# Masks of a routed MLP as a penalty in PSUM instead of a multiplication, and the order of one batch's products

## The chip, the cores and the metric

The kernel runs on one core of a Trainium2 chip. The metric is the device time of one execution in microseconds; several executions are timed and their median is given. The profile comes from one further execution.

## The reference, cut to what matters

The input is x, 4 batches of 256 tokens with 256 features, and a context of 4 x 256 x 64. Two layers follow, each an attention and an MLP, each added to x through a tanh gate. The change touches the first layer's MLP and what stands around it:

```python
# first layer, attention: adjacency from the context
A = sigmoid(sim) * (sim >= 76th largest of its row)
A = (A + A.T) * 0.5                      # mixed with the identity, applied to layernorm(x)
# first layer, MLP: 16 blocks of 64 hidden units, each token keeps its best 4 blocks
prob = softmax(xf @ Wr.T + br)
mask = 1 at the 4 largest of 16, else 0  # per token
h = gelu(xf @ W1b) * mask[:, :, None]
y = h @ W2b
x = x + tanh(g_ffn[0]) * y
```

The second layer is a latent attention over 16 heads, done in pairs of heads, and a mixture of experts. Neither is edited.

## The kernel before, in words

The program is written out by hand for each engine: each has one queue of instructions in program order, and semaphores join them. A batch b (0 to 3) has two tiles of 128 tokens.

VectorE (lines 888 to 960) runs, for each batch, ten rounds on the similarity of the context, MAX8 (line 908) and MATCH_REPLACE8 (line 913), to find the 76th largest value of each row, and then writes the thresholded A (line 936), which raises `a_ok`. Between the rounds of batch b it does the rest of the work of earlier batches, at fixed rounds: `first(b-1)` (line 823, adds the attention to x and takes the statistics), `norm_inverse` and `norm_apply` (lines 90 and 98, write XN), `second(b-2)` (line 855, adds the MLP's y), `route(b-1)` (lines 837 to 847, writes the mask MK, 1 where a block is among the best four), and `rest` (line 864).

TensorE does, for batch b: `result(b-1, 0..3)`, the MLP's second product of the previous batch (line 630, accumulated in the bank YB, raises `y_ps`); `norm_turn`, the transpose of XN (line 107); the logits (line 665); four units, each the hidden values of four blocks, two times 128 of them, by 256 tokens (line 674, f32, eight matmuls), written in turn to two banks; behind each unit the masks of the unit before (line 613): for each of the four blocks a column of MK is spread over 64 columns as the stationary operand, the moving one is the f16 identity, and so a full mask of 128 x 512 comes out in the bank MB, eight f16 matmuls of 128 columns. Then `symmetric(b+1)`, the transposed sum A + A.T of the next batch (lines 589 and 590, waits for `a_ok`), the masks of the last unit, and for b of 1 and 2 `second_norm(b-1)`. In the last batch the products of the next attention stand between the units: `first_queries(k)` for k of 0 to 2 (line 243), `second_norm(2)` after the second unit and `result(3, n-2)` behind the third and fourth.

ScalarE takes each unit through the gelu (line 774) to one of two buffers GL in SBUF and copies each mask from PSUM to one of two buffers MS (line 781). In between stand the square roots of the norms (line 83), which need another table than the gelu, so that tables are loaded (ACT_TABLE_LOAD) four times in a batch.

POOL multiplies GL by MS into HT (line 481), 128 x 512 values a unit; HT is what the second product reads. In the last batch it also adds the rotated halves of the queries (`add_partners`, line 276), each behind one of these products. SyncE issues the swaps that these additions wait for (lines 267 and 268) once VectorE has rotated a group (`rotate_query`, lines 256 and 257).

After the last result TensorE does the first context product (lines 284 and 286), `next_fold(0)` (line 143), the turn of batch 3, `next_fold(1)`, and the attention begins.

## Time and profile before

| | us |
|---|---|
| median of 3 executions | 461.74 |
| lowest, highest | 461.54, 463.14 |
| profiled execution: its time | 463.19 |
| its span | 461.3 |
| TensorE busy | 435.8 (94%) |
| VectorE busy | 303.1 (66%) |
| ScalarE busy | 252.4 (55%) |
| POOL busy | 194.3 (42%) |

Views of the profile give times in us from the start of the span. PE is TensorE, PEld its weight loads, DVE VectorE, ACT ScalarE, SPq the queue of SyncE. A line of a timeline has the start, the time covered, the engine, the source line, the operation, output and inputs, shapes and the count of instructions merged into it (x8). Merged matmuls start one behind the other while their ends overlap, so the distance to the next start tells the cost. In square brackets stands the idle time before the line and what ended it. The program names buffers by their tensor: `wide` holds A, SIM and XA; `kc`, `ks`, `CT` and `XT` are also GL and MS here; `turned` and `HT` are the two buffers HT.

### The profile page before, as it was taken

The page shows a single profiled execution, that of the slowest core. Times are in us where ns is not written, and L with a number is a line of the kernel's source. Part 1 is how long each engine was busy: PE and PEld are TensorE (multiplying, and loading weights), DVE is VectorE, ACT ScalarE, POOL GpSimd, SP SyncE. Part 2 cuts the span into 40 slices and gives each one's busy share as a digit, 9 for nine tenths or more (in the row PEclk, how much of TensorE's full clock was granted, in tenths as well). Part 3 has the DMA queues.
Part 4 walks back from the last instruction along what each step waited for, and adds up shares of the span by engine and source line. Part 5 has one row for each costly group of instructions (what it writes and reads, how often), then busy time and mean ns, then how long its engine had stood idle before and what let it go on. Part 6 is the DMA issues. An engine that isn't in the chain of part 4 may idle for free. (4 is left out here: it accounts for less than half of the span.)

```text
span 461.3 us, 8845 instructions
## 1 busy us (share of the span) xinstructions
PE 435.8 (94%) x2723; PEld 278.3 (60%) x2723; DVE 303.1 (66%) x880; ACT 252.4 (55%) x629; POOL 194.3 (42%) x195
## 2 busy tenths in 40 slices
PE   5898998889988999999999999999999999989997
PEld 2586876777744555556555556555467784644476
DVE  3989799965247757677666677767744548546613
ACT  3584445444344776767677766677667342145510
POOL 1641404040434556555465754565643433744000
PEclk9995999999999999999999999999999988999999
DMA  7643000000204343442334333212200399889212
GB/s 243 195 122 87 25 0 2 1 1 7 64 0 99 77 101 82 97 119 66 93 77 107 92 73 98 59 43 58 70 23 2 111 309 312 227 183 274 74 36 92
DMA packets 61464, 43.81 MB, mean 95 GB/s; under 512 B 22971, under 2 KB 54518, under 8 KB 61430
## 3 DMA queue, kind: packets, MB, share of 16 engines
q1 hardware_dynamic: 60662, 41.04, 33.8%
q0 software_dynamic: 768, 2.36, 2.5%
q8 instruction: 17, 0.28, 0.2%
q14 instruction: 17, 0.14, 0.1%
HBM read 27.25 MB, written 2.23 MB: 64 GB/s over the span
## 5 line engine op out<-in xcount | busy, mean ns | idle before, releaser
L1208 POOL TENSOR_TENSOR W1T<-W1T,inv 128x512 f32<-128x512 f32 x64 | 66.5, 1040 | 79.4 <-DVE inv L1263 79.4
L1152 ACT ACTIVATE W1T<-ps,low 128x256 f32<-128x256 f32 x128 | 59.5, 470 | 30.8 <-DVE low L1257 30.8
L276 POOL TENSOR_TENSOR rot<-rot 128x512 f32<-128x512 f32 x48 | 61.0, 1271 | 26.7 <-DMA rot<-rot 26.7
L1257 DVE TENSOR_REDUCE low<-ps 128x2 f32<-128x512 f32 x64 | 44.1, 689 | 39.1 <-PE ps L1067 38.6
L1160 ACT ACTIVATE W2T<-ps 128x512 f32<-128x512 f32 x64 | 38.2, 597 | 7.2 <-PE ps L1075 5.2
L1075 PEld LDWEIGHTS ps<-ident,W1T 128*128 128x128 f32 x256 | 27.8, 141 | 23.7 <-issue 20.7
L1075 PE MATMUL ps<-ident,W1T 128*128 128x128 f32 x256 | 41.1, 283 | 0.9 <-POOL W1T L1208 0.8
L256 DVE TENSOR_TENSOR rot<-ps,sinq 128x512 f32<-128x512 f32 x48 | 33.2, 691 | 13.4 <-PE ps L243 11.2
L243 PE MATMUL ps<-XH,CH 128*128 128x512 f16 x96 | 36.4, 379 | 0.9 <-DVE XL L864 0.9
L243 PE MATMUL ps<-XL,CH 128*128 128x512 f16 x96 | 36.4, 379 | 0.0
L243 PE MATMUL ps<-XH,CL 128*128 128x512 f16 x96 | 36.4, 379 | 0.0
L1084 PE MATMUL ps<-W2T,KV 128*64 128x256 f32 x256 | 34.7, 392 | 0.0
L674 PE MATMUL ps<-XT,W1T 128*128 128x256 f32 x128 | 33.3, 410 | 0.0
L257 DVE TENSOR_TENSOR rot<-ps,cosq 128x512 f32<-128x512 f32 x48 | 32.6, 680 | 0.0
L1067 PE MATMUL ps<-KL,Q 128*128 128x256 f16 x128 | 31.4, 273 | 0.0
L1067 PE MATMUL ps<-KH,Q 128*128 128x256 f16 x128 | 31.4, 273 | 0.0
L674 PEld LDWEIGHTS ps<-XT,W1T 128*128 128x128 f32 x128 | 25.4, 205 | 4.3
L908 DVE MAX8 m<-work 128x8 f32<-128x256 f32 x72 | 26.7, 412 | 0.0
L913 DVE MATCH_REPLACE8 work<-m,work 128x256 f32<-128x256 f32 x64 | 25.7, 408 | 0.0
L1152 ACT ACTIVATION_READ_ACCUMULATOR W1T<-ps,low 128x1 f32 x128 | 25.3, 198 | 0.0
L134 PE MATMUL ps<-NH,wide 128*128 128x256 f16 x128 | 23.1, 273 | 1.0 <-PEq L1987 0.8
L1263 DVE RECIPROCAL inv<-tot 128x2 f32<-128x2 f32 x64 | 10.1, 158 | 19.5 <-ACT W1T L1152 19.5
(247 smaller groups left out, 883.5 us busy)
## 6 DMA issues: line engine op xcount, KB each, us to landing
rot<-rot SPq DMA_DIRECT2D x64, 128.0 KB, 2.3
rot<-rot SPq DMA_DIRECT2D x64, 64.0 KB, 2.0
EGU<-in_L_ffn_W_gate_dram SPq DMA_DIRECT2D x8, 384.0 KB, 6.0
EGU<-in_L_ffn_W_up_dram SPq DMA_DIRECT2D x8, 384.0 KB, 6.1
ED<-in_L_ffn_W_down_dram SPq DMA_DIRECT2D x8, 384.0 KB, 6.0
rot<-in_L_ffn_W_dram SPq DMA_DIRECT2D x2, 1024.0 KB, 10.1
WQ<-in_L_xattn_Wq_dram SPq DMA_DIRECT2D x8, 256.0 KB, 3.0
WO<-in_L_xattn_Wo_dram SPq DMA_DIRECT2D x8, 256.0 KB, 3.1
```

Of the source, the lines that this page charges most:

```text
L243: mm = pe.matmul(g.ps[:, bank, :], cx[:, c, x * P:(x + 1) * P], xx[:, c, 512 * n:512 * n + 512], start=(c == 0 and m == 0), stop=(c == KT ...
L256: dve.tensor_tensor(batches(g.TS[x][:, :]), src, over(g.sinq), ALU.mult).then_inc(g.sin_ok, 1)
L257: dve.tensor_tensor(batches(g.TC[x][:, :]), src, over(g.cosq), ALU.mult).then_inc(g.rope_ok, 1)
L276: pool.tensor_tensor(g.RO[:, n, x, :], g.RO[:, n, x, :], g.TC[x][:, :], ALU.add).then_inc(g.sum_ok, 1)
L674: mm = pe.matmul(g.ps[:, HB + u % 2, S * o:S * o + S], W1T[:, k, (2 * n + o) * P:(2 * n + o + 1) * P], XT[b % 2][:, k, :], start=(k == 0), ...
L1067: mm = pe.matmul(g.ps[:, SC + t % 2, S * h:S * h + S], g.Q[h][u][:, t * P:(t + 1) * P], kx[:, S * (t // 2):S * (t // 2) + S], start=(m == ...
L1075: mm = pe.transpose(g.ps[:, PTB, j * P:(j + 1) * P], PB[t % 2][:, j // 2, (j % 2) * P:(j % 2 + 1) * P], g.ident[:, :])
L1084: mm = pe.matmul(g.ps[DC * h:DC * h + DC, CXB, 0:S], g.KV[:, 2 * b + j, 0, :], PTS[b % 2][:, 2 * h + j, :], start=(j == 0), stop=(j == 1))
L1152: e = act.activation(PB[t % 2][:, h, :], g.ps[:, SC + t % 2, h * S:(h + 1) * S], ACT.Exp, bias=low[:, t % 2, h:h + 1], scale=-1.0, accum_o ...
L1160: act.activation(PTS[t // 2 % 2][:, :, (t % 2) * P:(t % 2 + 1) * P], g.ps[:, PTB, :].rearrange("p (j n) -> p j n", j=4), ACT.Copy).then_in ...
L1208: pool.tensor_tensor(PB[t % 2][:, :, :], PB[t % 2][:, :, :], inv[:, t % 2, :].unsqueeze(2).broadcast_to([P, 2, S]), ALU.mult).then_inc(nor ...
L1257: dve.tensor_reduce(low[:, t % 2, :], g.ps[:, SC + t % 2, :].rearrange("p (h s) -> p h s", h=2), AX.X, ALU.min).then_inc(low_ok, 1)
```

## The change

The masks no longer become tensors of the units' size. MK is now 1 where a block is left out (`is_equal`). `turn_masks` transposes it with two small f16 matmuls to 16 x 256 (blocks by tokens), ScalarE copies that to OUT, and `mask(b, n)` adds to a unit, still in PSUM, two f16 matmuls with 16 rows, PENALTY times OUT: -32768 where the block is left out. The gelu of that is zero, and ScalarE writes it straight to HT. PENALTY is made once by one activation at ScalarE's start. Units lie in four banks (1, 2, 3 and 0; in the last batch the fourth takes bank 1 again), and the gelus follow the four penalties. POOL's products go, and `add_partners` stands alone at its end. In batch 0 the second transposed sum stands in front of the fourth unit. In the last batch units, queries and results are in a new order. On ScalarE the root of the second norm moves in front of the gelus, and an activation of one value loads the Gelu table ahead of the masks.

```diff
@@ -324,7 +324,9 @@
     work = sb("work", [P, 2, S])
     m8 = sb("m8", [P, 2, ROUNDS, 8])
     raw = sb("raw", [P, 5])
-    primed = sb("exp_primed", [1, 1])
+    primed = sb("tables", [1, B + 1])
+    PENALTY = sb("PENALTY", [NBLK, HID], F16)
+    OUT = sb("OUT", [NBLK, S], F16)
     gam = sb("gam", [P, 4])
     mix = sb("mix", [P, 3, NT])
     w1 = g.rot[:, 0:4, :].rearrange("p a (b d) -> p (a b) d", b=2)
@@ -349,9 +351,6 @@
     RP = sb("RP", [P, NT, FILL + NBLK])
     M8 = sb("M8", [P, NT, 8])
     MK = sb("MK", [P, NT, NBLK], F16)
-    pairs_of = lambda x: x[:, :, :].rearrange("p (a t) d -> p a (t d)", a=2)
-    GL = [pairs_of(kc), pairs_of(ks)]
-    MS = [pairs_of(CT), spare[:, 4:6, :]]
     HT = [turned[:, :, :].rearrange("p a (o s) -> p (a o) s", s=S), sb("HT1", [P, HID // P, S])]
 
     kcoli = sb("kcoli", [P, NT], mybir.dt.int32)
@@ -392,7 +391,9 @@
             eng.wait_ge(emptied, plain(n))
 
 
-    HB, MB, AB, TB, UB, YB = 1, 3, 4, 5, 6, 7
+    AB, TB, UB, YB = 4, 5, 6, 7
+    hid_bank = lambda b, n: (1, 2, 3, 0 if b < B - 1 else 1)[n]
+    MASKED_OUT = -32768.0
     UNITS = HID // P // 2
 
     @block.sync
@@ -472,14 +473,6 @@
             pool.tensor_scalar(XA[:, t, :], g.X[:, t, :], mix[:, 1, t:t + 1], mix[:, 2, t:t + 1],
                                ALU.mult, ALU.add).then_inc(xa_ok, 1)
 
-        def masked(b, n):
-            u = UNITS * b + n
-            pool.wait_ge(gelu_ok, u + 1)
-            pool.wait_ge(ms_ok, u + 1)
-            if b >= 2:
-                pool.wait_ge(y_ps, b - 1)
-            pool.tensor_tensor(HT[b % 2][:, 2 * n:2 * n + 2, :], GL[u % 2][:, :, :], MS[u % 2][:, :, :],
-                               ALU.mult).then_inc(ht_ok, 1)
         def fold_second(k):
 
             r, f = k // FOLDS, k % FOLDS
@@ -492,11 +485,8 @@
 
         for k in range(FOLDS):
             fold_second(k)
-        for b in range(B):
-            for n in range(UNITS):
-                masked(b, n)
-                if b == B - 1 and n >= 1:
-                    add_partners(pool, g, 0, n - 1)
+        for k in range(QT):
+            add_partners(pool, g, 0, k)
 
     @block.tensor
     def _(pe):
@@ -600,19 +590,33 @@
                 pe.wait_ge(g.d_w[r], DW)
             fold_product(pe, g, r, f, fold_bank(k)).then_inc(filled, 1)
 
+        def turn_masks(b):
+
+            pe.wait_ge(mk_ok, b + 1)
+            for j in range(2):
+                mm = pe.matmul(g.ps[0:NBLK, TB, j * P:(j + 1) * P], MK[:, 2 * b + j, :], g.ident16[:, :],
+                               start=True, stop=True)
+            mm.then_inc(mask_ps, 1)
+
+        def unit(b, n):
+
+            if b >= 1:
+                pe.wait_ge(gelu_ok, UNITS * b + n - UNITS + 1 if n < UNITS - 1 or b < B - 1 else UNITS * b + 1)
+            for o in range(2):
+                for k in range(KT):
+                    pe.matmul(g.ps[:, hid_bank(b, n), S * o:S * o + S],
+                              W1T[:, k, (2 * n + o) * P:(2 * n + o + 1) * P], XT[b % 2][:, k, :],
+                              start=(o == 0 and k == 0), stop=False, skip_group_check=True)
+
         def mask(b, n):
 
-            pe.wait_ge(mk_ok, b + 1)
-            if UNITS * b + n >= 1:
-                pe.wait_ge(ms_ok, UNITS * b + n)
+            pe.wait_ge(ms_ok, b + 1)
+            pe.wait_ge(pen_ok, 1)
             for o in range(2):
-                for j in range(2):
-                    for c in range(2):
-                        block_no = 2 * (2 * n + o) + c
-                        pick = MK[:, 2 * b + j, block_no:block_no + 1].broadcast_to([P, BLK])
-                        mm = pe.matmul(g.ps[BLK * c:BLK * c + BLK, MB, S * o + j * P:S * o + (j + 1) * P],
-                                       pick, g.ident16[:, :], start=True, stop=True)
-            mm.then_inc(mask_ps, 1)
+                mm = pe.matmul(g.ps[:, hid_bank(b, n), S * o:S * o + S],
+                               PENALTY[:, (2 * n + o) * P:(2 * n + o + 1) * P], OUT[:, :],
+                               start=False, stop=True, skip_group_check=True)
+            mm.then_inc(h_ps, 1)
 
         def second_norm(b):
             if b >= 1:
@@ -622,7 +626,7 @@
         def result(b, n):
 
 
-            pe.wait_ge(ht_ok, UNITS * b + n + 1)
+            pe.wait_ge(gelu_ok, UNITS * b + n + 1)
             if b >= 1 and n == 0:
                 pe.wait_ge(x2_ok, 2 * b)
             for j in range(2):
@@ -645,6 +649,8 @@
             pe.wait_ge(xl_ok, 2)
             pe.wait_ge(fold_b, 2)
             pe.wait_ge(g.rope_ok, k + ROPE0)
+            if k == 0:
+                pe.wait_ge(gelu_ok, UNITS * (B - 1))
             query_product(pe, g, 0, k, QA)
 
         pe.wait_ge(id_ok, 2)
@@ -655,6 +661,8 @@
             for n in range(UNITS):
                 if b >= 1:
                     result(b - 1, n)
+            if b >= 1:
+                pe.wait_ge(ms_ok, b)
             norm_turn(pe, g, n1, b, g.ps[:, TB, :]).then_inc(xt_ps, 1)
             pe.wait_ge(xt_ok, b + 1)
             if b == 0:
@@ -665,29 +673,33 @@
                     mm = pe.matmul(g.ps[:, AB, j * NBLK:(j + 1) * NBLK], XT[b % 2][:, k, j * P:(j + 1) * P],
                                    WrT[:, k, :], start=(k == 0), stop=(k == KT - 1))
             mm.then_inc(lg_ps, 1)
-            for n in range(UNITS):
-                u = UNITS * b + n
-                if u >= 2:
-                    pe.wait_ge(gelu_ok, u - 1)
-                for o in range(2):
-                    for k in range(KT):
-                        mm = pe.matmul(g.ps[:, HB + u % 2, S * o:S * o + S],
-                                       W1T[:, k, (2 * n + o) * P:(2 * n + o + 1) * P],
-                                       XT[b % 2][:, k, :], start=(k == 0), stop=(k == KT - 1))
-                mm.then_inc(h_ps, 1)
-                if n >= 1:
-                    mask(b, n - 1)
-                if b == B - 1 and n == 1:
+            if b < B - 1:
+                for n in range(UNITS - 1):
+                    unit(b, n)
+                turn_masks(b)
+                if b == 0:
+                    symmetric(b + 1)
+                unit(b, UNITS - 1)
+                for n in range(UNITS):
+                    mask(b, n)
+                if b >= 1:
+                    symmetric(b + 1)
                     second_norm(b - 1)
-                if b == B - 1 and n < QT:
-                    first_queries(n)
-                if b == B - 1 and n >= 2:
-                    result(b, n - 2)
-            if b < B - 1:
-                symmetric(b + 1)
-            mask(b, UNITS - 1)
-            if 1 <= b < B - 1:
-                second_norm(b - 1)
+        b = B - 1
+        unit(b, 0)
+        first_queries(0)
+        unit(b, 1)
+        unit(b, 2)
+        turn_masks(b)
+        second_norm(b - 1)
+        for n in range(UNITS - 1):
+            mask(b, n)
+        first_queries(1)
+        unit(b, UNITS - 1)
+        mask(b, UNITS - 1)
+        result(b, 0)
+        first_queries(2)
+        result(b, 1)
         result(B - 1, UNITS - 2)
         result(B - 1, UNITS - 1)
         pe.wait_ge(gelu_ok, UNITS * B)
@@ -719,6 +731,10 @@
             act.activation(SIM[:, 2 * b:2 * b + 2, :], o, ACT.Copy).then_inc(sim_ok, 1)
             act.activation(SIG[:, 2 * b:2 * b + 2, :], o, ACT.Sigmoid).then_inc(emptied, 1)
 
+        act.wait_ge(id_ok, 2)
+        act.activation(PENALTY[:, :].rearrange("p (n d) -> p n d", n=NBLK),
+                       g.ident16[0:NBLK, 0:NBLK].unsqueeze(2).broadcast_to([NBLK, NBLK, BLK]), ACT.Copy,
+                       scale=MASKED_OUT).then_inc(pen_ok, 1)
         context(0)
         act.activation(GT[:, :], bank(N_G)[0:DC, 0:DC], ACT.Copy).then_inc(emptied, 1)
         projection(0)
@@ -767,18 +783,19 @@
             fold_keep(act, g, 1, 1, f, g.ps[:, YB, :]).then_inc(g.attention.fold_hi, 1)
 
         def gelu(b, n):
-            u = UNITS * b + n
-            act.wait_ge(h_ps, u + 1)
-            if u >= 2:
-                act.wait_ge(ht_ok, u - 1)
-            act.activation(GL[u % 2][:, :, :], g.ps[:, HB + u % 2, :], ACT.Gelu).then_inc(gelu_ok, 1)
-            if n == 0 and b >= 1:
-                norm_root(act, g, n2, b - 1)
-
-        def mask(b, n):
-            u = UNITS * b + n
-            act.wait_ge(mask_ps, u + 1)
-            act.activation(MS[u % 2][:, :, :], g.ps[:, MB, :], ACT.Copy).then_inc(ms_ok, 1)
+            act.wait_ge(h_ps, UNITS * b + n + 1)
+            if b == 1 and n == 0:
+                act.wait_ge(iotf_ok, 2)
+            if b >= 2 and n == 0:
+                act.wait_ge(y_ps, b - 1)
+            act.activation(HT[b % 2][:, 2 * n:2 * n + 2, :], g.ps[:, hid_bank(b, n), :], ACT.Gelu
+                           ).then_inc(gelu_ok, 1)
+
+        def masks(b):
+
+            act.activation(primed[:, b:b + 1], g.gate[0:1, 0:1], ACT.Gelu)
+            act.wait_ge(mask_ps, b + 1)
+            act.activation(OUT[:, :], g.ps[0:NBLK, TB, 0:S], ACT.Copy).then_inc(ms_ok, 1)
 
         def second_norm(b):
             act.wait_ge(x2t_ps, b + 1)
@@ -797,20 +814,21 @@
                 norm_root(act, g, n1, b)
             act.wait_ge(xt_ps, b + 1)
             act.activation(XT[b % 2][:, :, :], g.ps[:, TB, :], ACT.Copy).then_inc(xt_ok, 1)
+            if b >= 1:
+                norm_root(act, g, n2, b - 1)
+            masks(b)
+            if b == B - 1:
+                second_norm(b - 1)
             for n in range(UNITS):
                 gelu(b, n)
-                if n >= 1:
-                    mask(b, n - 1)
-                if n == UNITS - 1:
-                    mask(b, n)
-                if b >= 1 and n == (2 if b == B - 1 else UNITS - 1):
-                    second_norm(b - 1)
+            if 1 <= b < B - 1:
+                second_norm(b - 1)
         norm_root(act, g, n2, B - 1)
         next_fold(0)
         second_norm(B - 1)
         next_fold(1)
         context_keep(act, g, 0, 0, 0)
-        act.activation(primed[:, :], g.gate[0:1, 0:1], ACT.Exp)
+        act.activation(primed[:, B:B + 1], g.gate[0:1, 0:1], ACT.Exp)
 
     @block.vector
     def _(dve):
@@ -845,7 +863,7 @@
                                   NEG).then_inc(mark_ok, 1)
             dve.wait_ge(mark_ok, 2 * b + 2)
             dve.tensor_tensor(MK[:, t, :], LG[:, t, FILL:], RP[:, t, FILL:],
-                              ALU.not_equal).then_inc(mk_ok, 1)
+                              ALU.is_equal).then_inc(mk_ok, 1)
 
         def second(b):
 
```

## Rows read from the trace of the kernel before

**Rows 1.** Windows of 12 us: busy and instructions by engine, granted clock, DMA.

```profile
core 0: us, PE busy (x) PEld busy (x) DVE busy (x) ACT busy (x) POOL busy (x), PEclk, DMA share, GB/s
...
36.00:48.00 12.00, 11.31 (x49) 8.44 (x49) 11.84 (x52) 4.39 (x8) 0.79 (x2) 0.57 0.40 101
...
120.00:132.00 12.00, 11.55 (x64) 8.20 (x62) 2.62 (x5) 3.60 (x6) 7.43 (x6) 1.00 0.12 31
```

**Rows 2.** TensorE in order of time, 47 to 98 us: start, us, instruction, idle before.

```profile
47.53 0.41 PE L613 MATMUL ps<-ident,MK 128*64 128x128 f16 x8
...
47.88 1.99 PE L674 MATMUL ps<-XT,W1T 128*128 128x256 f32 x8
...
52.41 0.49 PE L589 MATMUL ps<-ident,wide 128*128 128x128 f32 x2
...
54.74 7.17 PE L630 MATMUL ps<-W2T,turned 128*128 128x256 f32 x32
...
97.69 0.49 PE L589 MATMUL ps<-ident,wide 128*128 128x128 f32 x2 [1.25 <-DVE wide L936]
```

**Rows 3.** TensorE in order of time, last batch and hand-over, 115 to 135 us.

```profile
115.37 0.63 PE L107 MATMUL ps<-ident,XN 128*128 128x128 f32 x4 [0.42 <-DVE XN L98]
...
129.24 1.99 PE L630 MATMUL ps<-W2T,HT 128*128 128x256 f32 x8 [0.45 <-POOL HT L481]
131.16 1.08 PE L284 MATMUL ps<-rot,M 128*64 128x512 f32 x4
...
134.71 0.63 PE L107 MATMUL ps<-ident,XN 128*128 128x128 f32 x4 [0.62 <-DVE XN L98]
```

**Rows 4.** VectorE in order of time, around batches 1 and 2.

```profile
54.50 0.88 DVE L823 SCALAR_TENSOR_TENSOR X<-ps,gam,wide 128x256 f32<-128x256 f32 x2 [3.25 <-PE ps L590]
...
59.68 0.15 DVE L90 RECIPROCAL rstd<-std 128x2 f32<-128x2 f32 x1
...
63.40 0.86 DVE L855 SCALAR_TENSOR_TENSOR X<-ps,gate,X 128x256 f32<-128x256 f32 x2
...
77.61 0.86 DVE L823 SCALAR_TENSOR_TENSOR X<-ps,gam,wide 128x256 f32<-128x256 f32 x2
```

**Rows 5.** TensorE in order of time, two f16 products of the attention.

```profile
143.96 0.28 PE L1067 MATMUL ps<-KH,Q 128*128 128x256 f16 x1
144.08 0.27 PE L1067 MATMUL ps<-KL,Q 128*128 128x256 f16 x1
```

**Rows 6.** ScalarE in order of time, 3 to 98 us.

```profile
4.92 0.59 ACT L710 ACTIVATE turned<-ps 64x512 f32<-64x512 f32 x1 [2.90 <-PE ps L514]
...
55.47 1.28 ACT L83 ACT_TABLE_LOAD   x1
...
92.22 0.60 ACT L774 ACTIVATE ks<-ps 128x512 f32<-128x512 f32 x1
```

**Rows 7.** VectorE, then POOL, in order of time, 70 to 98 us.

```profile
70.86 1.49 DVE L98 TENSOR_SCALAR XN<-X,mv,rstd 128x256 f32<-128x256 f32 x2
...
72.94 1.87 DVE L936 SCALAR_TENSOR_TENSOR wide<-wide,m 128x256 f32<-128x256 f32 x2
...
95.77 1.87 DVE L936 SCALAR_TENSOR_TENSOR wide<-wide,m 128x256 f32<-128x256 f32 x2
...
73.20 1.32 POOL L481 TENSOR_TENSOR HT<-ks,XT 128x512 f32<-128x512 f32 x1 [1.32 <-ACT XT L781]
```

**Rows 8.** Source lines 98 and 936: shortest, median, longest ns, first and last start.

```profile
L98 DVE TENSOR_SCALAR XN<-X,mv,rstd x18: 403/410/1167, 36.4 to 375.5; 128x256 f32<-128x256 f32 x18
...
L936 DVE SCALAR_TENSOR_TENSOR wide<-wide,m x8: 461/480/1484, 26.8 to 96.2; 128x256 f32<-128x256 f32 x8
```

**Rows 9.** SyncE's queue in order of time, last swap issue of group 2.

```profile
124.21 0.58 SPq L268 DMA_DIRECT2D rot<-rot  x1
```

**Rows 10.** DMA issues of the page: KB each, us to landing.

```profile
rot<-rot SPq DMA_DIRECT2D x64, 64.0 KB, 2.0
```

**Rows 11.** Windows of 2 us, TensorE alone: busy, granted clock, DMA.

```profile
34.00:36.00 2.00, 0.41 (x4) 1.00 0.17 37
...
46.00:48.00 2.00, 2.00 (x15) 0.87 0.44 131
```

6 lines of the change are left out of this document (3 added, 3 removed).

## Prediction, made before the change was run

> **What bounds the kernel now.** I read the stretches first, then each engine's instructions in order of time. Until about 98 us VectorE is full (11.84 of 12 us in the first of [rows 1]), with the rounds of MAX8 and MATCH_REPLACE8 and the other VectorE work threaded between them. From then to 131 us it is TensorE (11.55 of 12 in the second). So the first layer has two legs: VectorE's chain up to the last A, which releases the fourth transposed sum at 97.69 [rows 2], and TensorE's queue from there to the first context product at 131.16 [rows 3]. What follows is bound by TensorE and is not edited; it should start earlier by the sum of both legs.
>
> In the VectorE timeline the one long hole is 3.25 us in front of 54.50 [rows 4]: the first update of batch 1 waits for the second transposed sum, which TensorE starts only at 52.41 [rows 2], behind four units and three mask groups.
>
> **Leg 1, the moved sum.** A is there from about 48.3 (the first rounds of batch 2 stand behind it), so TensorE's place alone decides. Out of its front go the fourth unit (1.9 us, from the row at 47.88) and three mask groups of 0.35 us (47.53 to 47.88) [rows 2]; in come two small transposes, 0.1 us. The sum starts 2.85 us earlier and ends near 51.6. VectorE stood ready at 54.50 - 3.25 = 51.25, so 2.9 us of the hole go.
>
> **What is late next.** TensorE still has to do all of batch 0 before y. New order: sum to 51.55, fourth unit 1.9, four pairs of penalty matmuls. The kernel has no such pair. The nearest row is an f16 matmul of 256 columns, started every 0.11 us [rows 5], so 0.22 a pair; the upper bound is twice that, the spacing at which f32 matmuls of that width go (8 in 1.9 us). I take 0.22, since operands and width are those of the f16 row: 0.9 for four, to 54.35. The first result waits for the first gelu, until 54.5, against 54.74 now [rows 2]; results take 7.0, y comes at 61.65. VectorE asks for it at 63.40 [rows 4] minus 2.9 = 60.5. It therefore waits 1.15 us and keeps a lead of 1.75. Within this also lies a new wait: the square root of the norm of batch 1, behind its table load of 1.28 [rows 6], stands behind four gelus in a row (53.85 to 55.9, each 0.60 with 0.1 overlap [rows 6]) and comes at 57.4; VectorE wants it at 59.68 - 2.9 = 56.8 [rows 4]. These 0.6 us are inside the 1.15, not beside them.
> The Trainium skill, "ScalarE: Activation LUTs", section What ACT_TABLE_LOAD costs, puts a switch of tables at 2.66 us, load and drain together. This trace shows 1.28 and no drain; by the page the lead would be 0.9, not 1.75.
>
> **Leg 1, POOL's products go.** Slow pairs stand out in VectorE's timeline: XN takes 1.49 at 70.86, A takes 1.87 at 72.94 and again at 95.77 [rows 7], where the medians of one are 0.41 and 0.48 [rows 8], 0.74 and 0.86 a pair. Each time POOL's mask product was running, as at 73.20 [rows 7]. The change deletes these products, and POOL has no other work here. Gain 0.75 + 1.0 + 1.0 = 2.75.
> The skill's "SBUF — State Buffer", section Who interferes with whom, says that a VectorE instruction with two SBUF inputs and a GpSimd one that reads SBUF exclude each other, and the later one blocks. These rows agree.
>
> Can TensorE follow? Batch 1: norm and logits to 63.7, three units, transposes, fourth unit, four penalty pairs: 72.05. A is ready at 72.94 + 1.87 - 3.5 = 71.3 (the later 1.0 of the 2.75 is still to come), so the sum runs 72.05 to 74.1, just when VectorE asks for it (the update of batch 2, 77.61 [rows 4] - 3.5 = 74.1). No margin, no wait. Batch 2: TensorE is free at 92.15 and A ready at 97.6 - 4.5 = 93.1. **Lead at the end of leg 1: 1.75 + 2.75 = 4.5 us**; TensorE idles 1.0 us there, as it does 1.25 now [rows 2].
>
> ScalarE loses 16 mask copies (0.6 each) and two table loads a batch. All that is off the path, except the copy of OUT in the last batch. The penalty table costs it about 1.05 us (0.60 for 512 columns, plus 512 more at the same rate) at 2.0 us of the kernel, and it idles until the first transposes release it at 4.92 [rows 6]: nothing. Without that cover it would cost 1.05. The new activations that only load the Gelu table run while ScalarE waits for masks: nothing.
>
> **Leg 2, TensorE's queue of the last batch.** Removed: mask groups of unit 2/3 and all of batch 3, 5 x 0.35 = 1.75; the wait for XN of batch 2, 0.42, since that turn now stands two units later; the wait for POOL's last product, 0.45 [rows 3]. Added: four pairs 0.9; transposes 0.1; the trip of the mask through ScalarE (0.4 for the copy and 0.2 around it), covered by the turn of batch 2 (0.46), 0.15 open. The fourth unit waits for the gelu of the first, long done behind 1.3 us of queries. Net -1.5. The third query product is now issued after result 0 and ends 5.7 us before the context product. Its rotation (0.7), four swap issues of 0.6 (the last as in [rows 9]), landing 2.0 [rows 10] and POOL's addition 1.3 (a product of the same size, [rows 7]), now with nothing ahead of it, take 6.4: context waits 0.7. The wait holds fold 0 and the turn of batch 3 behind it; that turn already waits 0.62 for XN [rows 3], so between nothing and 0.7 remains, and I take 0.2. **Leg 2: -1.3 us.**
>
> **Sum.** 4.5 + 1.3 = 5.8. The profiled execution took 463.19 (span 461.3): 457.4 for a run like it. The median shown is 1.45 lower; the same 5.8 off 461.74 is **455.9**. A measurement here tells 0.5%, 2.3 us, from no change.
>
> **Rivals.**
> 1. VectorE's slow rows stay: POOL was not their cause. For it: only coincidence in time is shown. Against: every slow pair has a POOL product over it, and the same instructions elsewhere do not vary. The lead stays 1.75, total 3.1: 458.6. Chance 0.08.
> 2. Penalty pairs cost 0.46, as f32 ones. Each batch 1 us later on TensorE: y of batch 0 takes 1.0 of the lead, the third sum another 1.0 (no margin), and TensorE then holds the fourth; with 0.9 in the last batch total 2.9: 458.8. Chance 0.06. Beside it, a table switch as the page prices it: 5.8 - 0.9 = 4.9, 456.8. Chance 0.03, since the load and the root behind it stand back to back.
> 3. The clock. In 34 to 36 us TensorE was busy 0.41 of 2 us at a full granted clock; over 36 to 48 the mean is 0.57 [rows 1], and it came back in 46 to 48 [rows 11]: (1 - 0.57) / 0.5 x 12 = 10.3 us at half (1.2 GHz), 5.2 us lost where TensorE is the bound. The idle of 1.25 at 97 caused no fall [rows 2]. If the shifted waits cause one such stretch between 92 and 125, the gain is 0.6: 461.1, no change. Chance 0.10. For it: the idle in front of the fourth sum, which grows to 3.7 if rival 1 holds. Against: in my sum TensorE idles less than now.
> 4. Slower: two such stretches, one from the fourth sum (93) and one from the hand-over at 131 to 136, where TensorE waits for norm and queries. Price 10.4, total +4.6: 466.3. It decides from 16 us at half clock (8.1 lost, 5.8 + 2.3). The hand-over keeps 2.4 GHz now with the same waits. Chance 0.04.
> 5. The moved sum does nothing, since y of batch 0 holds VectorE entirely (results as late as 63.4): leg 1 is 2.75, total 4.0: 457.7. Chance 0.06; TensorE's queue would have to grow by 1.75 for it.
>
> **How the numbers follow.** The forecast has the remaining 0.63. Its own range: 453.9, if nothing of the 2.9 is given back and pairs are free, up to 457.2. The range must leave out at most 2 in 10: rivals 1, 2 and 5 are taken in, with 1.4 us for the scatter between executions (461.54 to 463.14), to 460.0; rivals 3 and 4 mostly stay outside. Low end 453.6. Faster by over 0.5% (below 459.4): forecast, rivals 1, 2, 5 nearly whole, 0.85. Same: rival 3 and a rest, 0.11. Slower: rival 4, 0.04.
>
> **What would show it.** The second transposed sum starts near 49.6 and VectorE's hole before its first update of batch 1 shrinks to under 0.5; a wait for y near 60.5 to 61.7 is new. The pairs of XN and A take 0.74 and 0.86 everywhere. The fourth sum starts near 93.2, the context product near 125.5 to 126.5, behind a wait for POOL's addition of under 1 us. Penalty matmuls start 0.11 apart. The clock shows one stretch at half before 100 us. I am wrong if the fourth sum starts after 96, if the slow pairs remain with POOL idle, if a second stretch at half clock appears, or if TensorE loses after 136 what it gained before.

## The result, and the profile after

| | before | after |
|---|---|---|
| median of 20 executions each, us | 462.28 | 459.83 |
| lowest, highest, us | 460.93, 464.22 | 457.18, 461.6 |
| ratio after / before, 95% interval | | 0.9936 [0.992, 0.9953] |
| profiled execution: time, span, us | 463.19, 461.3 | 460.09, 458.1 |

The kernel is faster by 0.64% (3.0 us; the interval is 2.2 to 3.7), where 5.8 us (1.26%) was forecast. The time lies inside the stated range, just below its upper end of 460.0, and the sign is right, but half of the expected gain is missing. Executions of one kernel differ by 3 to 4 us, and the slower ones have the lower mean granted clock.

The page of the changed kernel, its span and the busy time of each engine:

```profile
span 458.1 us, 8618 instructions
PE 435.2 (95%) x2635; PEld 278.8 (61%) x2635; DVE 299.6 (65%) x880; ACT 238.8 (52%) x616; POOL 174.2 (38%) x179
```

POOL, ScalarE and VectorE are relieved of 20, 14 and 3.5 us. TensorE, which sets the end, is busy as long as before (435.8, in both with the stretches at half clock in it). Of the 3.2 us between the two spans, 2.6 are idle time of TensorE that is gone (25.5 us before, 22.9 after).

TensorE's timeline of the changed kernel, batch 0 and the second transposed sum (L579 and L580 are the sum, L607 a unit, L597 the turn of the mask, L616 the penalties, L634 the results; lines between those shown are left out):

```profile
48.95 0.28 PE L597 MATMUL ps<-ident,MK 128*16 128x128 f16 x2
49.16 0.49 PE L579 MATMUL ps<-ident,wide 128*128 128x128 f32 x2
51.05 1.89 PE L607 MATMUL ps<-XT,W1T 128*128 128x256 f32 x8
52.88 1.04 PE L616 MATMUL ps<-OUT,PENALTY 16*128 16x256 f16 x8
53.95 0.48 PE L634 MATMUL ps<-W2T,turned 128*128 128x256 f32 x1
```

The second sum is at 49.16 instead of 52.41 [rows 2], ahead of the fourth unit. Eight penalty matmuls take 53.95 - 52.88 = 1.07 us, 0.27 a pair.

VectorE's timeline of the changed kernel, the rows that answer to [rows 4] and [rows 7]:

```profile
51.26 0.88 DVE L841 SCALAR_TENSOR_TENSOR X<-ps,gam,wide 128x256 f32<-128x256 f32 x2
56.91 0.17 DVE L90 RECIPROCAL rstd<-std 128x2 f32<-128x2 f32 x1 [0.70 <-ACT std L83]
61.16 0.88 DVE L873 SCALAR_TENSOR_TENSOR X<-ps,gate,X 128x256 f32<-128x256 f32 x2 [0.43 <-PE ps L634]
...
68.64 0.74 DVE L98 TENSOR_SCALAR XN<-X,mv,rstd 128x256 f32<-128x256 f32 x2
69.95 0.87 DVE L954 SCALAR_TENSOR_TENSOR wide<-wide,m 128x256 f32<-128x256 f32 x2
...
90.38 0.74 DVE L98 TENSOR_SCALAR XN<-X,mv,rstd 128x256 f32<-128x256 f32 x2
91.69 0.86 DVE L954 SCALAR_TENSOR_TENSOR wide<-wide,m 128x256 f32<-128x256 f32 x2
```

The hole of 3.25 us [rows 4] is gone (51.26 carries no idle time). Behind it stand two new waits, 0.70 for the root and 0.43 for y. (In the second and third profile of the changed kernel, whose first unit starts about 1 us earlier, only the 0.43 is left.) XN and A take 0.74 and 0.87 everywhere, where they took up to 1.49 and 1.87 [rows 7].

ScalarE's timeline behind the units of batch 0, gelus, table load and root:

```profile
53.30 2.06 ACT L791 ACTIVATE turned<-ps 128x512 f32<-128x512 f32 x4 [3.66 <-PE ps L616]
55.38 1.28 ACT L83 ACT_TABLE_LOAD   x1
56.68 0.20 ACT L83 ACTIVATE std<-var 128x2 f32<-128x2 f32 x1
```

The root follows the load after 0.02 us and the load the last gelu likewise: no drain is seen.

TensorE's timeline around the fourth transposed sum, and the stretches with busy time and granted clock there (columns: stretch, its length, busy us and matmuls, granted clock, DMA share, GB/s):

```profile
90.55 1.04 PE L616 MATMUL ps<-OUT,PENALTY 16*128 16x256 f16 x8
92.61 0.49 PE L579 MATMUL ps<-ident,wide 128*128 128x128 f32 x2 [1.01 <-DVE wide L954]
...
93.60 0.52 PE L579 MATMUL ps<-ident,wide 128*128 128x128 f32 x2
93.92 0.64 PE L580 MATMUL ps<-wide,ident 128*128 128x128 f32 x2
```

```profile
90.00:92.00 2.00, 1.59 (x11) 1.00 0.00 0
92.00:94.00 2.00, 1.39 (x11) 0.93 0.00 0
94.00:96.00 2.00, 2.00 (x11) 0.50 0.00 0
96.00:98.00 2.00, 2.00 (x9) 0.72 0.00 0
```

The sum starts at 92.61 instead of 97.69 [rows 2]. But the granted clock falls to 0.50 (1.2 GHz) one us later: a pair of the sum takes 0.64 instead of 0.39. In the profile of before an idle of 1.25 us at the same place was followed by no such fall [rows 2].

TensorE's timeline of the last batch, up to the attention (L243 are queries, L284 the context product, L107 the turn, L143 the folds), and then POOL's last addition and SyncE's last swap issue:

```profile
113.15 0.82 PE L616 MATMUL ps<-OUT,PENALTY 16*128 16x256 f16 x6
113.91 0.39 PE L243 MATMUL ps<-XH,CH 128*128 128x512 f16 x1
...
120.47 5.34 PE L634 MATMUL ps<-W2T,HT 128*128 128x256 f32 x24
127.23 1.08 PE L284 MATMUL ps<-rot,M 128*64 128x512 f32 x4 [1.41 <-issue]
...
131.34 0.92 PE L143 MATMUL ps<-WCQ,WQ 128*128 128x192 f32 x4 [0.74 <-DVE CL L187]
```

```profile
125.87 1.26 POOL L276 TENSOR_TENSOR rot<-rot 128x512 f32<-128x512 f32 x1 [5.47 <-DMA rot<-rot]
```

```profile
123.63 0.69 SPq L268 DMA_DIRECT2D rot<-rot  x1
```

The context product waits 1.41 us. POOL's addition ends at 125.87 + 1.26 = 127.13, just ahead of it: in this view "issue" hides a wait for POOL.

**Where the time went, by legs.** To keep the early stretch out, I measure from the start of the first unit. The table has that start, the leg to the fourth transposed sum, the leg from there to the context product, both together, and the tail from the last turn (line 107) to the end. All four profiles of either kernel are there (the repeats are described below). The part between, from the context product to the last turn, is 244.9 in all eight.

| profile | first unit | leg 1 | leg 2 | both | tail |
|---|---|---|---|---|---|
| before | 41.35 | 56.34 | 33.47 | 89.81 | 85.24 |
| before, second | 39.39 | 55.23 | 33.47 | 88.70 | 85.19 |
| before, third | 41.34 | 55.99 | 33.47 | 89.46 | 85.49 |
| before, fourth | 40.04 | 56.35 | 33.47 | 89.82 | 85.31 |
| after | 41.33 | 51.28 | 34.62 | 85.90 | 85.96 |
| after, second | 40.49 | 50.91 | 32.95 | 83.86 | 86.75 |
| after, third | 40.22 | 51.09 | 34.59 | 85.68 | 85.79 |
| after, fourth | 41.39 | 51.50 | 34.68 | 86.18 | 86.93 |

The means: the first unit +0.33, leg 1 -4.78 (so the fourth sum stands 4.46 us earlier), leg 2 +0.74, tail +1.05, together -2.7. Over all timed executions the means are 462.09 (136 executions of before) and 459.30 (37 of after), -2.8. The missing gain is in leg 2 and in the tail, not in leg 1.

The clock has a third place to fall, which the views above do not show. In windows of 2 us the granted clock is 0.50 again in the expert stage, from about 377 to 384 us in three of four profiles of before and from about 374 to 381 in two of four of after (the first and fourth); in the second of after it is from 371 to 375 and from 399 to 402. It costs little there: in before the tail is 85.24, 85.49 and 85.31 with the stretch and 85.19 without it. TensorE has slack at that place, as the profile without the stretch waits 1.78 us for VectorE at 384.16. So the mean granted clock of an execution mixes stretches that cost time with one that hardly does.

### The profile page after: what moved, and what is told of

It reads as the page before. It is cut to its first block and busy times, and to the rows that moved or that the text cites. A ratio compares the mean times of both kernels' runs of the same rounds, so it can differ in the third digit from the quotient of the medians.

```text
span 458.1 us, 8618 instructions
## 1 busy us (share of the span) xinstructions
PE 435.2 (95%) x2635; PEld 278.8 (61%) x2635; DVE 299.6 (65%) x880; ACT 238.8 (52%) x616; POOL 174.2 (38%) x179
## 5 line engine op out<-in xcount | busy, mean ns | idle before, releaser
L243 PE MATMUL ps<-XH,CH 128*128 128x512 f16 x96 | 36.4, 379 | 0.1
L243 PE MATMUL ps<-XL,CH 128*128 128x512 f16 x96 | 36.4, 379 | 0.0
L243 PE MATMUL ps<-XH,CL 128*128 128x512 f16 x96 | 36.4, 379 | 0.0
L1102 PE MATMUL ps<-W2T,KV 128*64 128x256 f32 x256 | 34.7, 392 | 0.0
L607 PE MATMUL ps<-XT,W1T 128*128 128x256 f32 x128 | 31.9, 404 | 0.0
L607 PEld LDWEIGHTS ps<-XT,W1T 128*128 128x128 f32 x128 | 25.4, 203 | 4.0
```

Of the source, the lines that this page charges most:

```text
L243: mm = pe.matmul(g.ps[:, bank, :], cx[:, c, x * P:(x + 1) * P], xx[:, c, 512 * n:512 * n + 512], start=(c == 0 and m == 0), stop=(c == KT ...
L607: pe.matmul(g.ps[:, hid_bank(b, n), S * o:S * o + S], W1T[:, k, (2 * n + o) * P:(2 * n + o + 1) * P], XT[b % 2][:, k, :], start=(o == 0 an ...
L1102: mm = pe.matmul(g.ps[DC * h:DC * h + DC, CXB, 0:S], g.KV[:, 2 * b + j, 0, :], PTS[b % 2][:, 2 * h + j, :], start=(j == 0), stop=(j == 1))
```

## The experiments

All are compared with before on the chip on which they ran. A repeated kernel says how far single profiles can be trusted.

### Repeats of both kernels

Edit: none, for each of the six.

> The changed kernel once more, unchanged, for a second profile and clocks beside those of the same chip. The half-clock stretch behind 93.6 is there again if it belongs to the schedule; the ratio to the kernel before is 0.993 again. From the last transpose of the norm (372.1) to the end 85.9 us again if the expert stage really became 0.7 us longer, 85.2 if that is scatter.

> The kernel before once more, unchanged. From its last norm transpose to its end the first profile has 85.24 us, eight profiles of other versions 85.9 to 86.8. If the expert stage is the same for both kernels and only scatters, this profile has about 86.1; if the change costs 0.7 us there, 85.2 again. From the fourth sum to the context product 33.5 us again, with no half-clock stretch at 97.

> The changed kernel a third time. One of two profiles has the stretch at half clock behind the fourth sum. With it the way from the fourth sum to the context product takes 34.6 us, without it 33.0; the rest of the program takes 244.9 and about 86 us either way.

> The kernel before a third time, for the same three lengths. The first stretch at half clock (36 to 46.8 in the first profile) may be shorter; the fourth sum is then up to 1 us earlier.

> The changed kernel, a fourth profile. Expert stage 85.8 or more if it is longer with this kernel; below 85.6 would make it scatter. Fourth sum to context product 33.0 without the half-clock stretch behind the sum, 34.6 with it; it came in two of three.

> The kernel before, a fourth profile. Last norm transpose to the end: 85.2 to 85.5 if the expert stage really is shorter with this kernel, 85.8 to 86.8 if the three values so far were the low end of one scatter. Fourth sum to context product 33.5.

Measured for before, run as its own variant: 0.9994 [0.9975, 1.0013], 0.9982 [0.9962, 1.0002], 0.9997 [0.9978, 1.0016]. For after: 0.9946 [0.9925, 0.9967], 0.9917 [0.9886, 0.9948] (3 executions only), 0.9927 [0.9906, 0.9947]. So after is faster by 0.5 to 0.8%, and each comparison sees it. Two things come out of the table above. Leg 2 of before is 33.47 in four of four profiles; leg 2 of after is 32.95 once and 34.6 to 34.7 three times, and these three have the stretch at half clock behind the fourth sum. The stretch costs 34.6 - 32.95 = 1.65 us, measured against a single profile without it. And VectorE's hole in before is 3.25, 0.65, 2.89 and 2.32 us, long when the early half-clock stretch is long. The second repeat of before, VectorE's first update of batch 1:

```profile
51.43 0.88 DVE L823 SCALAR_TENSOR_TENSOR X<-ps,gam,wide 128x256 f32<-128x256 f32 x2 [0.65 <-PE ps L590]
```

The hole that I took as a fixed 3.25 belonged partly to the execution that was profiled.

### The moved sum alone

Before, with only the second sum moved; run twice.

```diff
             for n in range(UNITS):
                 u = UNITS * b + n
+                if b == 0 and n == UNITS - 1:
+                    symmetric(b + 1)
...
-            if b < B - 1:
+            if 1 <= b < B - 1:
                 symmetric(b + 1)
```

> The kernel before with only the second transposed sum ahead of batch 0's fourth unit. Forecast's theory (VectorE's hole closes, but the wait for y of batch 0 takes most of it back): the hole of 3.25 us falls to about 1.3 (three mask groups less two stand in front of the sum), y is still near 61.9, the fourth sum starts near 96.2 instead of 97.69, the time falls by 1.5 us. Rival (TensorE's place of the sum was all that mattered): the fourth sum starts near 95 and the time falls by 2.5 or more. Rival (the sum does nothing): fourth sum within 0.3 us of 97.69.

> The kernel before with only the moved sum, a second profile. Its last stage is word for word that of before: below 85.6 again if the stage follows the kernel, so that its 85.93 was a chance value. Slow A at 47 (POOL's product falls on it) if the early stretch at half clock ends by 45.

Measured: 462.49 us, ratio 1.0007 [0.999, 1.0024]; again 462.77, 1.0011 [0.9993, 1.003]. Legs 56.29 + 33.47 and 56.21 + 33.47: as before. The move alone gives nothing; the 1.5 us that were expected of it do not come. Its VectorE rows, and POOL's, show why:

```profile
47.08 1.87 DVE L938 SCALAR_TENSOR_TENSOR wide<-wide,m 128x256 f32<-128x256 f32 x2
...
61.61 0.48 DVE L857 SCALAR_TENSOR_TENSOR X<-ps,gate,X 128x256 f32<-128x256 f32 x1 [1.15 <-PE ps L630]
```

```profile
47.26 1.42 POOL L481 TENSOR_TENSOR turned<-kc,CT 128x512 f32<-128x512 f32 x1 [8.74 <-ACT CT L783]
```

The hole is gone here too, but A itself now meets a product of POOL and takes 1.87 instead of 0.86, and y is waited for 1.15. Together 2.2 us, about what the hole was worth in an execution with this early stretch (2.32 in the fourth profile of before, whose first unit is at 40.04, here 40.02; there POOL's product starts 0.4 us behind A and not 0.2, and A keeps 0.86). The second profile shows the same, A 1.87 and the wait for y 1.14. Both have the first unit at 40.0 or just below: where the move's gain goes in an execution with the long early stretch was not profiled, only that the 20 timed executions show none.

### The sum moved back, in the changed kernel

```diff
                 turn_masks(b)
-                if b == 0:
-                    symmetric(b + 1)
                 unit(b, UNITS - 1)
...
+                symmetric(b + 1)
                 if b >= 1:
-                    symmetric(b + 1)
                     second_norm(b - 1)
```

> The changed kernel with the second transposed sum behind batch 0's penalties. If the sum's place is worth 1.8 us of the lead, the fourth sum starts near 94.5 instead of 92.61 and the time rises by 1.8 us. If the deleted POOL products carry the lead alone, it stays within 0.3 us. A side effect the clock theory allows: the idle ahead of the fourth sum becomes longer, and with it the stretch at half clock behind it.

Measured: 461.40 us, 0.9981 [0.9957, 1.0004]. Its update of batch 1 on VectorE and its fourth sum on TensorE:

```profile
54.53 0.88 DVE L839 SCALAR_TENSOR_TENSOR X<-ps,gam,wide 128x256 f32<-128x256 f32 x2 [3.13 <-PE ps L580]
```

```profile
94.46 0.80 PE L579 MATMUL ps<-ident,wide 128*128 128x128 f32 x2 [1.59 <-DVE wide L952]
```

The hole is back, 3.13. Leg 1 is 52.96, against 56.34 and 55.99 in before and 51.28 and 51.50 in after (all with the first unit at 41.3 to 41.5). So without the move, the deleted products and all else are worth 3.0 to 3.4 us of leg 1, and the move 1.6 on top. The mean time is 1.8 us above that of after (461.12 against 459.30), as expected. Half clock follows this sum too (leg 2 34.59), and the tail is 86.08: of the lead, 1.1 us go in leg 2 and 0.8 in the tail, and what is left against before, 0.9 us, is within the noise. With POOL quiet the move is worth something; alone it is not: the two parts need each other.

### POOL's load put back

The changed kernel, with five products of the old size on POOL in each of two batches, over buffers that nobody reads. This adds work and removes none.

```diff
+        flat = lambda x: x[:, :, :].rearrange("p t d -> p (t d)")
+        for u in range(10):
+            pool.wait_ge(mk_ok, u // 5 + 2)
+            pool.tensor_tensor(flat(kc), flat(ks), flat(CT), ALU.mult).then_inc(kv_sum, 1)
+            pool.wait_ge(kv_sum, u + 2)
```

> The changed kernel with five products of 128x512 on POOL from the mask of batch 1 on and again from the mask of batch 2 on, on idle buffers, waited for by nobody in the first layer. If POOL's reads of SBUF block VectorE's two-input instructions, XN and A of both stretches are slow again (pairs of 1.5 to 1.9 instead of 0.74 and 0.86), and the fourth sum starts 2 to 3.5 us later than 92.61. If the slow rows of before had another cause, XN and A keep 0.74 and 0.86 and the fourth sum stays at 92.6.

Measured: 465.33 us, 1.0083 [1.0053, 1.0113]. VectorE's XN and A in both batches, and POOL:

```profile
68.95 2.55 DVE L98 TENSOR_SCALAR XN<-X,mv,rstd 128x256 f32<-128x256 f32 x2
72.09 1.28 DVE L959 SCALAR_TENSOR_TENSOR wide<-wide,m 128x256 f32<-128x256 f32 x2
...
93.57 2.62 DVE L98 TENSOR_SCALAR XN<-X,mv,rstd 128x256 f32<-128x256 f32 x2
96.77 1.28 DVE L959 SCALAR_TENSOR_TENSOR wide<-wide,m 128x256 f32<-128x256 f32 x2
```

```profile
66.04 6.65 POOL L491 TENSOR_TENSOR kc<-ks,CT 128x512 f32<-128x512 f32 x5 [26.58 <-DVE MK L870]
90.72 6.66 POOL L491 TENSOR_TENSOR kc<-ks,CT 128x512 f32<-128x512 f32 x5 [18.03 <-DVE MK L870]
```

The cause of the slow rows is POOL: 0.74 becomes 2.55 and 2.62, 0.87 becomes 1.28, just where POOL runs, while MAX8 between them keeps its 0.74. The fourth sum comes 5.5 us later than in after (98.11 against 92.61), behind an idle of 3.08 us, and half clock follows it here too. It also follows the third sum, behind an idle of 1.41. The sizes were not as expected: XN suffers more than the 1.5 to 1.9 that were expected, A less, and the delay is more than 2 to 3.5. Five products in a row run here, where before had one at a time. Rival 1 is out.

### The idle before the fourth sum filled

The changed kernel; the first result of batch 2 goes ahead of the fourth sum.

```diff
+                if b == B - 2:
+                    result(b, 0)
                 if b >= 1:
                     symmetric(b + 1)
...
-                if b >= 1:
+                if b >= 1 and not (b == B - 1 and n == 0):
                     result(b - 1, n)
```

> The changed kernel with the first result product of batch 2 ahead of the fourth transposed sum, into TensorE's idle 1.01 us. Clock theory (the idle there is what lets the granted clock fall at 93.6): no stretch at half clock near 94, the context product's predecessors 1.0 (idle filled) and 1.5 us (clock) earlier, time lower by 1 to 2.5 us. Rival (the clock falls there for another reason): the half-clock stretch stays and the gain is 1.0 at most. Rival (VectorE's update of batch 3 becomes late because its sum is 0.8 us later): the turn of XN waits, gain below 0.5.

Measured: 457.19 us, 0.9891 [0.9864, 0.9918]. TensorE and its granted clock:

```profile
91.69 1.99 PE L634 MATMUL ps<-W2T,turned 128*128 128x256 f32 x8
93.53 0.39 PE L579 MATMUL ps<-ident,wide 128*128 128x128 f32 x2
```

```profile
92.00:94.00 2.00, 2.00 (x13) 1.00 0.00 0
94.00:96.00 2.00, 2.00 (x20) 1.00 0.00 0
```

No idle, no half clock. Both legs together are 83.30: 2.4 to 2.9 less than the profiles of after with the stretch, 0.56 less than the one without.

### The third queries ahead of the first result

The changed kernel; then the same on top of the filled idle.

```diff
         mask(b, UNITS - 1)
-        result(b, 0)
         first_queries(2)
+        result(b, 0)
         result(b, 1)
```

> The changed kernel with the third query product ahead of the first result of batch 3. If the swap's trip (rotation, four issues, landing, POOL's addition: 6.5 us after the queries end) is what context waits 1.41 us for, the wait disappears, since a result of 1.8 us comes between. The hand-over behind it is bound by the norm of batch 3 from 130.0 on, so of the 1.41 us 0.5 to 1.0 reach the attention. Rival (the wait is the norm's anyway): context starts earlier and the first fold turn waits as long more, gain 0.

> Both orders: first result of batch 2 ahead of the fourth sum and the third query product ahead of the first result of batch 3. The two gains lie one behind the other on TensorE's queue and should add: time about 0.984 to 0.988 of the kernel before. If the end of the expert stage is held by its weight loads and not by TensorE, the second gain shows at 370 us and not at the end.

Measured: 456.42 us, 0.9888 [0.9868, 0.9907], and with the filled idle 455.78, 0.9881 [0.9854, 0.9908]. TensorE in the first of the two:

```profile
117.49 7.07 PE L634 MATMUL ps<-W2T,HT 128*128 128x256 f32 x32
124.49 1.08 PE L284 MATMUL ps<-rot,M 128*64 128x512 f32 x4
...
128.03 0.63 PE L107 MATMUL ps<-ident,XN 128*128 128x128 f32 x4 [0.61 <-DVE XN L98]
```

The context product no longer waits, and the turn waits 0.61 for XN again, as before [rows 3]. Leg 2 is 33.06 with the half-clock stretch in it, 1.55 under the 34.6 of after; on top of the filled idle it goes from 31.11 to 29.57, 1.54. So the whole 1.4 us of the wait is on the path, where 0.5 to 1.0 had been expected.

### The penalty operands padded to 128 rows

The changed kernel; PENALTY and OUT get 128 rows, of which 112 are zero. The penalties have the same sum, but every row of TensorE takes part. Run twice.

```diff
-    PENALTY = sb("PENALTY", [NBLK, HID], F16)
-    OUT = sb("OUT", [NBLK, S], F16)
+    PENALTY = sb("PENALTY", [P, HID], F16)
+    OUT = sb("OUT", [P, S], F16)
...
+        pool.memset(OUT[:, :], 0.0).then_inc(kv_sum, 1)
+        pool.memset(PENALTY[:, :], 0.0).then_inc(kv_sum, 1)
...
-            act.activation(OUT[:, :], g.ps[0:NBLK, TB, 0:S], ACT.Copy).then_inc(ms_ok, 1)
+            act.activation(OUT[0:NBLK, :], g.ps[0:NBLK, TB, 0:S], ACT.Copy).then_inc(ms_ok, 1)
```

> The changed kernel with PENALTY and OUT padded with zeros to 128 rows, so that each penalty product works all rows of the array in the same 0.11 us. If the chip counts the 16-row products ahead of the idle 1.01 us as little work and this is why the clock falls there and did not before with a longer idle, the half-clock stretch at 94 disappears and the time falls by 1 to 1.5 us. If the idle time alone decides, the stretch stays and the time is that of the changed kernel.

> The changed kernel with the penalties padded to 128 rows, again. If the 16 rows in front of the idle are what lets the clock fall, this profile has no half-clock stretch near 93, the runs stay at a mean clock of 0.988 or more, and the time is 1 us or more below the changed kernel. If the first result was chance, it has the stretch like two of three profiles of the changed kernel.

Measured: 457.61 us, 0.9913 [0.9893, 0.9932]; again 457.65, 0.9913 [0.989, 0.9937]. TensorE and its granted clock:

```profile
89.03 1.04 PE L618 MATMUL ps<-OUT,PENALTY 128*128 128x256 f16 x8
91.35 0.49 PE L581 MATMUL ps<-ident,wide 128*128 128x128 f32 x2 [1.28 <-DVE wide L957]
```

```profile
90.00:92.00 2.00, 0.71 (x6) 1.00 0.00 0
92.00:94.00 2.00, 2.00 (x19) 1.00 0.00 0
94.00:96.00 2.00, 2.00 (x11) 1.00 0.00 0
```

The penalties take the same time and the idle is even longer (1.28), yet the clock stays at 1.00 in both profiles. Count the cases with the sum at its place and an idle of 1.0 to 1.3 us: behind 16-row products the clock fell in 4 of 5 profiles (three of after, and the early queries; not in the second of after), behind 128-row products in none of 8 (1.24 to 1.31 us; four of before and two of the moved sum alone, where the masks have 128 rows, and these two). The other idles agree: behind 16-row products it fell after 1.41, 1.59 and 3.08 us too (POOL's load back, the sum moved back) and not after 0.85 (third sum, the sum moved back), and behind 128-row masks it did not fall after the 1.24 to 1.25 us ahead of the third sum, in four of four profiles of before. That both padded profiles start their first unit at 40.0 does not explain them: the early queries (39.95) and the third of after (40.22) start there as well, and fell. But the padded kernel itself has only two profiles. In the timed runs the granted clock over a whole execution is 0.981 or less in 22 of 37 executions of after, in 9 of the 116 of before for which it is on record, and in none of 12 with padded rows (0.985 to 0.992). This count alone proves little, as it holds the expert stage's stretch too: the third profile of after has 0.989 and the fall behind the fourth sum, the kernel with filled idle and early queries has 0.981 without it. The mean time falls from 459.30 to 457.64, by 1.66 us. A stretch of 1.65 in about three of four executions would explain 1.2 of it. The rest is about the 0.4 to 0.5 by which leg 2 of the padded profiles (32.55, 32.41) is shorter even than that of after without the stretch (32.95); the next experiment shows where that comes from.

### All three together

> Penalties padded to 128 rows, first result of batch 2 ahead of the fourth sum, third query product ahead of the first result of batch 3. If rows and idle are two causes of the same half-clock stretch, the padding adds nothing to the other two: ratio 0.985 to 0.988 of the kernel before. If low array use also brings stretches elsewhere in the first layer, it is below 0.985.

The edit is the sum of the three above. Measured: 454.88 us, 0.9834 [0.9806, 0.9863]; 7.7 us under before, the fastest kernel here; its mean of 454.98 is 4.3 under that of after. The context product starts at 122.18 and does not wait.

The first unit and both legs, of the changed kernel and its variants:

| kernel | first unit | leg 1 | leg 2 | both | tail |
|---|---|---|---|---|---|
| sum moved back | 41.50 | 52.96 | 34.59 | 87.55 | 86.08 |
| POOL's load back | 41.40 | 56.71 | 34.30 | 91.01 | 85.87 |
| idle filled | 41.34 | 52.19 | 31.11 | 83.30 | 86.17 |
| queries early | 39.95 | 51.48 | 33.06 | 84.54 | 86.09 |
| filled and early | 41.46 | 52.18 | 29.57 | 81.75 | 86.09 |
| 128 rows | 40.04 | 51.31 | 32.55 | 83.86 | 86.50 |
| 128 rows, again | 40.02 | 51.21 | 32.41 | 83.62 | 85.93 |
| all three | 41.47 | 51.51 | 29.20 | 80.71 | 86.28 |

In the kernels with the filled idle, leg 1 contains the result that was moved into it, so that "both" is the number to compare. The padded rows give 1.04 us on top of the other two (81.75 to 80.71), where no half-clock stretch behind the fourth sum was left to remove. Set side by side, the two traces show where: 0.18 in the early stretch, which ends sooner in this execution, and the rest in steps of 0.05 to 0.1 us, nearly all where TensorE goes from 128-row products to 16-row ones or back. The fourth unit of batch 1, for one, takes 1.93 us from its start to that of the penalties in the first (68.91 to 70.84) and 1.84 in the second (68.64 to 70.48). So a block of 16-row products costs 0.1 to 0.3 us more than the same block with 128 rows, at its borders.

## Why the prediction was right or wrong

**The moved sum: right, with a condition that I had not seen.** Forecast: 2.9 of the hole go, 1.15 come back as waits, lead 1.75. In the profile the two waits are 0.70 + 0.43 = 1.13, with the root's part of the sum as forecast, and against the kernel with the sum moved back the lead is 1.6. But alone the move is worth nothing: in both profiles of it A then meets POOL's product. And the hole varies from 0.65 to 3.25 between executions of before. One profile was read as if it were all of them.

**POOL's products: right, somewhat low.** Forecast 2.75; the changed kernel with the sum moved back has 3.0 to 3.4 of leg 1, with all that else was changed in it. The cause was shown in both directions: products out, rows short; products in, rows up to 3.5 times as long. The rule of the Trainium skill, "SBUF — State Buffer", section Who interferes with whom, agrees for A, which has two SBUF inputs. XN has a single tensor input and suffers more (0.74 to 2.55), so that the two-input rule does not account for it; no run here tells what does.

**Leg 1 as a whole: right.** The fourth sum stands 4.46 us earlier in the mean of four profiles, forecast 4.5; 5.1 in the one profile of each that I first compared. That it comes so close is partly luck: measured from the first unit the leg is 4.78 shorter, and the first unit, which scatters by 2 us, happens to stand 0.33 later in the mean.

**Penalty pairs: slightly low.** 0.27 instead of 0.22, 0.25 in the last batch (six in 113.91 - 113.15 = 0.76). That is 0.2 us a batch, and the borders of the 16-row blocks, 0.1 to 0.3 us a block, were no term of the sum. Rival 2 (0.46) is out. So is a table switch of 2.66 us as the Trainium skill, "ScalarE: Activation LUTs", section What ACT_TABLE_LOAD costs, has it: the trace shows 1.28. ScalarE is rid of six table loads in all, not of two a batch; it is off the path either way.

**Leg 2: wrong, in two steps.** Forecast -1.3, measured +0.74.

The first is the sentence "that turn already waits 0.62 for XN, so between nothing and 0.7 remains, and I take 0.2". The context product waits 1.41, not 0.7. The results between the last query product and it take 5.3 us, not 5.7, and the way of the query through rotation, swap and addition 127.13 - 120.47 = 6.7, not 6.4. And all of it counts. The turn indeed waits no more, but right behind it fold 1 waits 0.74 for CL, a wait that the earlier kernel did not need to show. I took slack at one instruction for slack of the chain. TensorE's queue itself became shorter by 33.47 - (32.95 - 1.39) = 1.9 (the profile without the stretch waits 1.39), more than the 1.5 forecast. Without the stretch leg 2 is therefore -0.5.

The second is rival 3's "Against: in my sum TensorE idles less than now". The idle is less, 1.01 against 1.25, and still half clock follows in 3 of 4 profiles. Length of idle alone was the wrong measure: what TensorE did before it differs. The last thing before the idle is now a block of 16-row products, and with these padded to 128 rows the clock stayed in two of two profiles. Price 1.65 us each time, 1.24 in the mean (-0.5 + 1.24 = +0.74). The rival was right in kind, but it was priced at 5.2 us after the long early stretch, and this one is short. "A second stretch at half clock" was also among the signs of being wrong, and it appeared.

**The tail: forecast 0, measured +1.05.** It lies in the expert stage, which is not edited; the prediction took it that what follows "should start earlier by the sum of both legs", and gave it no term. All 12 profiles of after and its variants have 85.8 to 86.9, the four of before 85.2 to 85.5. But the kernel with the moved sum alone, whose code there is that of before, has 85.93 and 84.99, so the whole tail does not tell the kernels apart. Its first part does. POOL fetches rows by index, and TensorE turns the first of them; without the late stretch at half clock these lines are, in the second profile of before (last turn at 373.01) and in the third of after (370.81):

```profile
400.31 0.81 PE L1624 MATMUL ps<-ident,XR 128*128 128x128 f32 x4 [0.78 <-DMA XR<-token_rows,idx]
```

```profile
399.27 0.78 PE L1642 MATMUL ps<-ident,XR 128*128 128x128 f32 x4 [1.94 <-DMA XR<-token_rows,idx]
```

The fetch is issued 22.1 to 22.9 us behind the last turn in every profile of every kernel. TensorE's first use of its rows stands 27.3 to 27.9 us behind that turn in all six profiles with the code of before (four of before, two of the moved sum alone) and 28.3 to 29.0 in all twelve of after and its variants. That is 0.8 of the 1.05 in the mean of four, and it follows the kernel; the remaining 0.26 scatters. Why the rows land later in the changed kernel is open.

**The sum.** -4.5 (leg 1, with the start) + 0.7 (leg 2) + 1.1 (tail) = -2.7, against -5.8: 2.0 us are missing in leg 2, 1.1 in the tail. The steps that failed are these: the context product's wait, mis-sized and taken as mostly covered by the turn; the clock behind the fourth sum, taken as safe because the idle is shorter; and the tail, put at nothing. The chance of 0.85 for faster by over 0.5% went the right way, but 0.64% stands just beyond that line. The case that came about, forecast mechanism plus a short stretch at half clock plus a full context wait, was not in my list, since I added each hazard alone to a sum that was otherwise right. The sign of leg 1 and its size were never in danger; the queue behind it was.

## What to carry to other kernels

When lead is won on one engine, follow the next two waits behind it and not one: slack seen at one instruction may be the same slack that the instruction behind it lives on. A replacement with 16 rows cost TensorE no less time here than one with 128, a little more at its borders, and was followed by half clock after the next short idle: try padding it with zeros, or fill the idle. And take a hole that depends on an early clock stretch from several profiles.

## What the runs showed of the hardware that I had not expected

- An idle of 1.0 us behind eight matmuls of 16 rows (1.07 us) was followed by half clock in 4 of 5 profiles, an idle of 1.24 to 1.31 us behind matmuls of 128 rows in 0 of 8 (0 of 12 with the third sum of before). The rows are what the padding changed. Why the rows matter, and why 1 in 5 escapes, is open.
- Between 128-row and 16-row matmuls about 0.1 us is lost at a change (a unit takes 1.93 us up to the 16-row penalties, 1.84 up to the same padded to 128 rows); eight penalties take 1.07 us either way.
- About 7 us at half clock in the expert stage cost the tail of before next to nothing: 85.24 to 85.49 us with them, 85.19 without.
- The stretch behind the fourth sum costs about 1.65 us. The early one, from about 36 us on, differs between executions of the same kernel: the first unit starts anywhere from 39.39 to 41.35 in before.
- A VectorE TENSOR_SCALAR pair of 128 x 256 f32 goes from 0.74 to 2.55 us beside continuous POOL products, a SCALAR_TENSOR_TENSOR pair from 0.87 to 1.28, and MAX8 not at all.
